# Order of the tiles in the second stage of a two-layer convolution block: taken in turns from six parts of the sorted sequence

## The reference

```python
s = relu(score)
q_s = clip(floor(s), 0, 5); q_b = q_s + 1          # KERNELS = (1, 3, 5, 7, 9, 11, 13)
frac_b = s - q_s; frac_s = q_b - s
y = frac_b * maxpool(v, KERNELS[q_b]) + frac_s * maxpool(v, KERNELS[q_s]) + v
out = x + y
```

## Time and profile before

| what | us |
|---|---|
| median of 3 runs | 4258.09 (4254.13 to 4260.08) |
| the profiled execution, its own time | 4254.8 |
| its span, first to last instruction | 4252.9 |
| first tile of the second stage starts on VectorE | 2617.4 |
| last tile of the second stage ends on VectorE | 4196.8 |
| VectorE busy in this stretch | 1454.7 |

### The profile page before, as it was taken

The page is one execution under the profiler, slowest core; times in us unless marked ns, Lnnn a source line. Parts: engine busy times, 40 slices in busy tenths (PEclk is TensorE's granted clock), DMA queues, the critical chain, the costliest instruction groups (busy, mean ns, idle before and its releaser), DMA issues. The chain is left out here.

```text
span 4252.9 us, 74568 instructions
## 1 busy us (share of the span) xinstructions
PE 3857.3 (91%) x23656; PEld 2157.9 (51%) x23657; DVE 3377.6 (79%) x3619; ACT 1679.9 (40%) x2835; POOL 1954.0 (46%) x1576
## 2 busy tenths in 40 slices
PE   4999999999999999999999985889999888888775
PEld 3666666666666666566666644333344333333332
DVE  5777777777777777777777657889988899999994
ACT  3445544444444445454544521432233222222222
POOL 3556555555555555555555531433333333333332
PEclk9999999999999999999999996999999999999888
DMA  5445455455445545544544334654577566554551
GB/s 191 155 163 176 165 174 175 145 178 181 158 162 175 178 141 184 176 164 156 201 156 164 112 129 91 259 195 179 203 281 297 229 257 242 235 237 198 214 201 78
DMA packets 252358, 782.08 MB, mean 184 GB/s; under 512 B 98150, under 2 KB 98150, under 8 KB 229990
## 3 DMA queue, kind: packets, MB, share of 16 engines
q1 hardware_dynamic: 219600, 417.85, 28.5%
q0 software_dynamic: 32288, 358.95, 21.3%
HBM read 428.22 MB, written 409.08 MB: 197 GB/s over the span
## 5 line engine op out<-in xcount | busy, mean ns | idle before, releaser
L1024 DVE TENSOR_TENSOR arena<-arena 128x2048 f32<-128x2048 f32 (+9 forms) x635 | 1454.8, 2320 | 134.8 <-PE psum L1378 45.3
L437 POOL TENSOR_TENSOR arena<-arena 128x512 f16<-128x512 f32 x512 | 650.2, 1275 | 858.1 <-ACT arena L580 857.1
L665 ACT ACTIVATE arena<-psum,arena 128x512 f32<-128x512 f32 x536 | 367.6, 687 | 1113.8 <-PE psum L1378 1103.8
L1374 PE MATMUL psum<-arena 128*128 128x512 f32 x1072 | 583.4, 627 | 226.0 <-issue 220.6
L1203 PE MATMUL psum<-arena 128*128 128x512 f16 x2048 | 776.1, 379 | 1.0 <-ACT arena L592 1.0
L446 POOL TENSOR_TENSOR arena<-arena 128x512 f32 (+1 forms) x512 | 639.9, 1271 | 297.1 <-ACT arena L592 291.5
L1205 PE MATMUL psum<-arena 128*128 128x512 f16 x2048 | 776.2, 379 | 0.0
L1204 PE MATMUL psum<-arena 128*128 128x512 f16 x2048 | 776.2, 379 | 0.0
L1180 PE MATMUL psum<-arena 128*128 128x256 f16 (+1 forms) x6344 | 713.9, 270 | 33.6 <-DVE arena L774 20.5
L578 ACT ACTIVATE arena<-arena,gbias,grstd 128x512 f32 (+1 forms) x512 | 413.7, 808 | 631.7 <-PE psum L1205 515.7
L1180 PEld LDWEIGHTS psum<-arena 128*128 128x128 f16 x6344 | 589.8, 99 | 118.7 <-DVE arena L774 28.5
(11 more groups left out here) (150 smaller groups left out, 3351.3 us busy)
## 6 DMA issues: line engine op xcount, KB each, us to landing
arena<-in_x SPq DMA_DIRECT2D x64, 2048.0 KB, 13.0
wide_planes<-arena SPq DMA_DIRECT2D x128, 1024.0 KB, 8.9
y_planes<-arena SPq DMA_DIRECT2D x64, 2048.0 KB, 7.7
arena<-arena SPq DMA_DIRECT2D x1536, 8.0 KB, 1.8
arena<-wide_planes,arena POOLq DMA_INDIRECT x72
arena<-plane_records,arena POOLq DMA_INDIRECT x67, 7.3
arena<-y_planes,arena POOLq DMA_INDIRECT x67, 10.4
out<-arena POOLq DMA_INDIRECT x67, 8.3
```

What stands on the lines that cost most here:

```text
L437: pool.tensor_tensor(gl[:, ct, slot], g32[:, ct % 2, :], gh[:, ct, slot], ALU.subtract).then_inc(s_gl, 1)
L1024: ins = dve.tensor_tensor(dst, a, b, ALU.max)
L1374: pe.matmul(dst, diag[:, s, 0, :], bufs[:, u, b * CW:(b + 1) * CW], start=True, stop=False)
```

## The change

`tnum[t]` was t. It is now t//6 + 12 (t mod 6): the sorted sequence of 72 tiles is cut into six parts of 12, and the columns take one tile from each part in turn. Both the table and the classes follow `tnum`, so each plane is still computed once. An assertion is added that 72 divides by 6.

```diff
@@ -93,7 +93,7 @@
     NPL = NC * P
     NT = -(-(NC + NCLS - 1) // BUFS) * BUFS
     COLS = min(8, NC // 2)
-    assert B >= 4 and (B - 2) % 7 == 0 and NC % (2 * COLS) == 0
+    assert NT % NCLS == 0 and B >= 4 and (B - 2) % 7 == 0 and NC % (2 * COLS) == 0
     nc.disable_value_cache = True
 
@@ -484,7 +484,10 @@
             pool.wait_ge(s_conv, B * CH * CT)
             pool.iota(plane_i.rearrange("p (n a) -> p n a", a=1), [[C, B], [P, CT]], base=0, channel_multiplier=1)\
                 .then_inc(s_iota, 1)
-            pool.iota(tnum_i, [[1, NT]], base=0, channel_multiplier=0).then_inc(s_iota, 1)
+
+
+            pool.iota(tnum_i.rearrange("p (b a) -> p b a", a=NCLS), [[1, NT // NCLS], [NT // NCLS, NCLS]], base=0,
+                      channel_multiplier=0).then_inc(s_iota, 1)
             pool.iota(lane_i, [[1, P]], base=0, channel_multiplier=0).then_inc(s_iota, 1)
```

## The result

The changed kernel takes 4412.22 us (median of 4 runs, 4405.45 to 4417.33), against 4257.85 us before (4254.13 to 4260.08). The ratio is 1.0362, with a 95% interval of 1.0343 to 1.0382. The forecast was 4418 us, range 4385 to 4445.

What follows compares the result with a forecast made beforehand. Second stage: VectorE bounds classes 3 to 5, TensorE class 2, waiting for data class 0. VectorE's tiles +172 us, the end -12, net +160 on 4254.8 gives 4415, as a median 4418 us; range 4385 to 4445.

Steps and rivals of the forecast that it cites:

- The sum: VectorE's second-stage tiles, summed over rounds 0 to 11: 1751.8 us against 1579.4 before, +172.
- Before class 1: VectorE, after a short class 0 tile, waits for TensorE's class 5 tile: 10.9 us.
- term P: TensorE's time for tile t-2, for which VectorE must wait; 23.4 us for class 5 after about 7 us idle.
- Before class 3: VectorE, after a class 2 tile, waits for TensorE's class 1 tile: 6.2 us.
- Loop tops: VectorE idles at every fourth tile's jump back, 2.4 us; covered before classes 0 and 2, paid before 4.
- Empty tiles: Four move to the middle; VectorE passes each at once, then idles 22.4 to 25.0 us for TensorE.
- The end: After VectorE's last tile, one empty tile is left instead of five: -12 us.
- third rival: Every change of class makes VectorE wait for code, 2.9 us each, 22 paid: 4482 us; chance 0.06.
- Balance works: First rival: long and short tiles even out, VectorE never waits for TensorE: 4187 us, faster; chance 0.05.
- empty tiles drain nothing: Second rival: VectorE fills their place with the next tile, bubbles shrink to 10.9 us: 4362 us; chance 0.05.
- The fourth: Rival: iota's dimensions swapped, so the sorted order or nearly so stays: 4258 us; chance 0.02.
- even load on the DMA engines: Sign for the first rival: turns would even out the DMA share, 0.45 to 0.70 by class before.

Runs made afterwards that it cites:

- classes in turns run: Kernel before with classes 0 and 1 alternating for the first 22 tiles, the rest sorted, empty tiles last: 4332.46 us, ratio 1.0167.
- two products: Changed kernel with TensorE's product for the smaller window left out for every class: 4308.55 us; the same in the kernel before: 4248.03 us.
- written out: VectorE's 72 tiles written out instead of a loop over four: kernel before 4214.20 us, changed kernel 4387.76, changed kernel with two products 4233.35.
- run with empty tiles last: Changed kernel's order, but with the five empty tiles at the end: 4347.21 us, ratio 1.0211 to the kernel before.
- sorted run with empty tiles between: Kernel before in sorted order, but with four of the five empty tiles at columns 47, 53, 59 and 65: 4337.18 us, ratio 1.0196.
- classes 3, 4, 5 in turns: Kernel before with classes 0, 1, 2 sorted as before and classes 3, 4, 5 alternating: 4257.71 us, ratio 0.9998.
- turns without loop: Changed kernel with VectorE's tiles written out instead of looped over: 4387.76 us, ratio 1.0304 to the kernel before.

## Why the prediction was right

**The sum.** The forecast's 1751.8 us for VectorE's tiles is 1752.0 in the profile. With the first stage 4.7 us later and the end 14.7 shorter, the span of the profiled execution grew by 162.6 us; by the medians the change costs 154 where 160 was forecast. That the tiles agree to 0.2 us is luck, since single terms were off in both directions: the first round took 140.4 us for 142.6, the next six 912.8 for 913.8, round 9 141.9 for 143.8, and round 10 140.2 for 136.3.

**Before class 1:** 10.9 forecast, 9.8 to 10.8 in the full rounds. The term P was too high: TensorE's class 5 tile took 23.2 us before the first of them and 22.5 to 22.6 before the others, and not the 23.4 taken from the earlier trace rows. The classes in turns run, 4332 for 4330, shows this wait by itself.

**Before class 3:** 6.2 forecast; 6.4 to 7.0 where no loop top came before. Where one stood before class 2 it was 5.4 us, and class 3's wait shrank to 1.1 to 1.4. That the stall takes up a loop top was right. In the round with a loop top of 7.7 us no wait was left before class 3.

**Loop tops:** mis-sized. I took 2.4 us from classes 4 and 5; before class 4 they are 3.4 in turns, and 6.3 with two products. In these traces their size moved between 1.1 and 7.7 us. It goes with the DMA share around the jump and not with the class: between class 4 tiles it is 2.5 to 2.8 us at shares up to 0.19 and 5.5 to 5.7 us at 0.84 to 0.87. The prediction had thought of the DMA share, but took the mean of the stage, 0.56, where the last 4.4 us of work and the loop top have 0.40 to 0.52 before class 4 in the full rounds and 0.85 and more before class 2. The cover that I named for those before classes 0 and 2 is real; written out, turns gain 24 us and sorted 44.

**Empty tiles:** 22.4 to 25.0 forecast, 24.0, 24.1, 25.5 and 25.3 in the profile. The wait for data behind the first two was 3.9 and 0.7 us for about 5 each; behind the third it was 2.1 where the sum had none, and class 4 behind two tiles of class 2 waited 5.7 for 4.0. The run with empty tiles last gives this part as 65 us, the sorted run with empty tiles between 79.

**The end:** -12 forecast, 56.1 - 41.4 = 14.7 shorter in the profile.

**A row misread.** The prediction puts the 5.28 us of the earlier trace rows at the border of class 0 to class 1 and makes them the one thing that speaks for its third rival. Class 1 begins a tile earlier, at 2796.70 by the earlier trace rows. The loop top at 2824.87 stands between two class 1 tiles, so it never was a row for a price of class changes. The forecast doesn't use it.

**The rivals.** "Balance works" is refuted by classes 0 and 1 in turns; "empty tiles drain nothing" by the run with them among the sorted tiles; "a change of class costs a fetch" by classes 3, 4, 5 in turns and, for the other classes, by the turns without loop. The fourth, an order other than computed, is out by the 58 operations of each round. The even load on the DMA engines, the one thing that speaks for the change, came, and the waits for data fell by about 5 us.

## What to carry to other kernels

Before mixing long and short tiles so that two engines even out, write down for one handover how far the first may run ahead. With two buffers its next start is the other's end of the tile before last, and a short tile behind a long one only makes the wait visible: sum over max(0, handover + P(t-2) - D(t-1)), with P the second engine's tile and D the first one's, not over averages. A tile that does nothing still takes its turn in the chain of waits and can cost as much as a full one, so keep such tiles at the end. And look at what is idle for "issue" at a fixed distance: a short loop on the bounding engine can cost more than an order of tiles can win.

## What the runs showed of the hardware that was not expected

VectorE's jump back in a loop of four tiles cost up to 7.7 us of idle time per pass, and how much went with the DMA share around the jump. Writing it out gained 44 us of 4258 in the sorted order, and 72 in turns with two products, where few waits for TensorE cover the loop tops. TensorE with two products per bank instead of three did not get faster in proportion: the mean granted clock of the whole run fell from 0.944 to 0.912 in turns, and most of its tiles took 15.4 to 17.1 us where 14.0 is the time at full clock. The tile at 2985.87, after 11.11 us of idle time, had a granted clock of 0.50 (1.2 GHz) in its first 3.5 us and 1.00 (2.4 GHz) later, and took 16.5 us; the one at 2960.76, after 2.07 us of idle time, had 1.00 throughout and took 14.0. So a part of what a product less saves is lost again at the lower clock.
